# ScalarE scales the expert rows, the second half's selection is spread out, and the last chunk's second layer runs by tokens

## What is computed

```
scores = (tanh(xf @ gate_w.T) + 1) / 2
vals, idx = top_k(scores.T, k)              # k = 1028 rows for each of 8 experts
y = layernorm(xf[idx]) * gamma + beta       # rows of 256
h = gelu(y @ fc1s.T + b1s)                  # 1024 wide
o = (h @ fc2s.T + b2s) * vals               # back to 256
out = xf; out[idx] += o
```

## Time and profile before

| what | us |
|---|---|
| timed runs, median of 3 (lowest, highest) | 770.85 (768.74, 771.48) |
| the profiled execution | 768.64 |
| its span, first to last instruction | 766.8 |
| TensorE busy | 692.5 (90% of the span) |
| VectorE busy | 521.9 (68%) |
| ScalarE busy | 461.3 (60%) |
| GpSimd busy | 475.5 (62%) |

### The profile page before, as it was taken

One profiled execution on the slowest core, in us unless ns is written; L12 is line 12 of the kernel. 1 busy time (PEld: TensorE's weight loads), 2 busy tenths in 40 slices (PEclk: granted clock), 3 DMA queues, 4 the chain that ended last, 5 costly groups with the idle time before them and its releaser, 6 DMA issues.

```text
span 766.8 us, 15683 instructions
## 1 busy us (share of the span) xinstructions
PE 692.5 (90%) x4636; PEld 636.4 (83%) x4636; DVE 521.9 (68%) x1827; ACT 461.3 (60%) x1095; POOL 475.5 (62%) x660
## 2 busy tenths in 40 slices
PE   6988999999999963528899999999999999999994
PEld 3977788888888853518798999999999999999993
DVE  2855789989889867988767674766746756534431
ACT  1002588888888878706456566665675666756651
POOL 0248598889889645435166586575775856658323
PEclk9979999999999995559999999999999999999998
DMA  9910012222222228312143253253442443433122
GB/s 257 307 32 1 5 58 81 82 83 82 82 82 83 83 82 156 113 44 97 15 97 92 45 116 100 45 131 64 104 98 50 103 104 69 119 50 64 15 28 28
DMA packets 63568, 64.19 MB, mean 84 GB/s; under 512 B 14032, under 2 KB 57104, under 8 KB 63376
## 3 DMA queue, kind: packets, MB, share of 16 engines
q1 hardware_dynamic: 50576, 46.33, 20.6%
q0 software_dynamic: 12800, 17.12, 13.7%
q10 hardware_dynamic: 128, 0.00, 0.0%
HBM read 37.90 MB, written 25.53 MB: 83 GB/s over the span
## 4 chain that ended last, share of the span: by engine, by line
PE 50%; DVE 5%; ACT 4%; issue 1%; POOL 1%; DMA 0%; POOLq 0%; ACTq 0%; DVEq 0%
PE bank L1043 23%; PE bank L1057 16%; PE bank L1069 6%; PE bank L1030 3%; ACT bank L753 2%; PE bank L1020 1%; DVE jk L1605 1%; ACT jk L753 1%; PE bank L1080 1%; DVE yl L1624 1%; ACT bank L763 1%; ACT hh L766 0%; DVE hl L1630 0%; DMA yg<-rows,idx 0%; DVE bank L1617 0%
## 5 line engine op out<-in xcount | busy, mean ns | idle before, releaser
L584 POOL DMA_INDIRECT out<-ob,sidx x72 | 117.0, 1625 | 144.7 <-ACT ob L779 126.3
L1630 DVE TENSOR_TENSOR hl<-bank,hh 128x384 fp32r<-128x384 f32 (+1 forms) x192 | 98.1, 513 | 147.2 <-ACT hh L766 123.7
L763 ACT ACTIVATE bank<-bank,b1s 128x384 f32<-128x384 f32 (+1 forms) x192 | 99.6, 519 | 147.6 <-PE bank L1043 130.9
L1043 PE MATMUL bank<-yh,w1h 128*128 128x384 f32 (+1 forms) x384 | 131.0, 341 | 0.1
L1043 PE MATMUL bank<-yh,w1l 128*128 128x384 f32 (+1 forms) x384 | 122.9, 320 | 0.0
L1043 PE MATMUL bank<-yl,w1h 128*128 128x384 f32 (+1 forms) x384 | 122.5, 319 | 0.0
L1057 PE MATMUL bank<-w2h,hh 128*128 128x256 f32 x384 | 108.7, 283 | 0.0
L1057 PE MATMUL bank<-w2h,hl 128*128 128x256 f32 x384 | 108.4, 282 | 0.0
L1057 PE MATMUL bank<-w2l,hh 128*128 128x256 f32 x384 | 108.4, 282 | 0.0
L558 POOL DMA_INDIRECT yg<-rows,idx x72 | 71.1, 987 | 42.1 <-DVE idx L1608 22.2
L766 ACT ACTIVATE hh<-bank 128x384 fp32r<-128x384 f32 (+1 forms) x192 | 87.9, 458 | 6.1
(11 more groups left out here) (248 smaller groups left out, 1770.6 us busy)
## 6 DMA issues: line engine op xcount, KB each, us to landing
BIG<-in_x SPq DMA_DIRECT2D x4, 2048.0 KB, 16.1
out<-Bs SPq DMA_DIRECT2D x32, 256.0 KB, 2.2
rows<-Yp SPq DMA_DIRECT2D x32, 256.0 KB, 2.4
raw<-in_fc1T SPq DMA_DIRECT2D x16, 512.0 KB
raw<-in_fc2T SPq DMA_DIRECT2D x16, 512.0 KB
yg<-rows,idx POOLq DMA_INDIRECT x72
out<-ob,sidx POOLq DMA_INDIRECT x72
gwb<-in_gate_w SPq DMA_DIRECT2D x1, 1024.0 KB, 7.1
```

What stands on the lines that cost most here:

```text
L584: g.indirect_dma_start(out=out_rows, out_offset=tok(ap=sidx[job.eh][0:m, t:t + 1], axis=0), in_=ob[t % 3][0:m, :], in_offset=None, compute ...
L763: A.activation(h[:, 0:cur.w], h[:, 0:cur.w], ACT.Gelu_apprx_tanh, bias=b1s[:, bass.ds(cur.e, 1), f]).then_inc(s["hact"], 1)
L1043: last = T.matmul(Lb[ring(cur, f)][:, 0:cur.w], w1s[cur.eh][i][:, d, f * P:(f + 1) * P], yT[cur.p][k][:, d, 0:cur.w], start=(n == 0), stop ...
L1630: v.tensor_tensor(hT[cur.p][1][:, f, 0:cur.w], Lb[ring(cur, f)][:, 0:cur.w], hT[cur.p][0][:, f, 0:cur.w], ALU.subtract).then_inc(s["hlo"], 1)
```

## The change

ScalarE's `high_rows` now also scales (an Identity with a scale and a bias column per partition, in place in the bank, then a wait for it), and VectorE's `scaled` is gone. Ahead of job 0 VectorE takes the low rows after tile 6, not after tile 5. The selection of the second half is spread over jobs 1 to 3; TensorE's two steps of it go to the end of jobs 1 and 2, into bank 3, and the waits that guarded bank 7 move from `place` to the turns of jobs 3 and 4, which write bank 3. The last expert's third chunk has its second layer by tokens (72 matmuls, no transposes back); the third chunks of the other experts stay as they were.

```diff
...
                 self.half, self.group = (self.q // 4, self.q % 4) if isinstance(self.q, int) else (1, self.q - 4)
                 self.q_next = not (isinstance(self.q, int) and self.q == NE - 1)
                 self.t0, self.t1 = CHUNKS[self.c]
+                self.by_tokens = self.c < 2 or not self.q_next
                 self.w = sum(SLOTS[self.t0:self.t1])
         def place_bank(job, t):
...
         def second(prev, f):
-            cut = CUT[3 if prev.c < 2 else 2]
+            cut = CUT[3 if prev.by_tokens else 2]
             return [(n // len(TERMS), n % len(TERMS)) for n in range(cut[f - 1] if f else 0, cut[f])]
         def ring(job, f):
...
                 after(act, "hmm", (job.j - 1) * 8)
                 for d in range(2):
+                    act.wait_ge(s["yt_t"], job.j * 2 + d + 1)
+                    A.activation(bank[2 + d][:, 0:job.w], bank[2 + d][:, 0:job.w], ACT.Identity, scale=gam[:, d:d + 1],
+                                 bias=bet[:, d:d + 1]).then_inc(s["yr"], 1)
                     act.wait_ge(s["yr"], job.j * 2 + d + 1)
                     A.activation(yT[job.p][0][:, d, 0:job.w], bank[2 + d][:, 0:job.w], ACT.Copy).then_inc(s["yhi"], 1)
...
             def weighed(prev, t):
                 m = SLOTS[t]
-                if prev.c < 2:
+                if prev.by_tokens:
                     act.wait_ge(s["oadd"], prev.q * 6 + t + 1)
                     src = ot[t % 2][0:m, :]
                 else:
...
                         high(1 - cur.eh, cur.q + 1, cur.c // 2, WHIGH_AT.index(f))
                     if nxt and f == HIGH_AT:
                         high_rows(nxt)
-                    if prev and prev.c < 2 and f in OB_AT:
+                    if prev and prev.by_tokens and f in OB_AT:
                         weighed(prev, prev.t0 + OB_AT.index(f))
-                    if prev and prev.c == 2 and f == BACK_AT:
+                    if prev and not prev.by_tokens and f == BACK_AT:
                         for t in range(prev.t0, prev.t1):
                             weighed(prev, t)
             act.wait_ge(s["ld_par"], 112)
...
                     pe.wait_ge(s["oh_first" if split else "ohd"], job.q + 1)
                 if t == 3 and split:
                     pe.wait_ge(s["ohd"], 1)
-                if t == 6 and isinstance(job.q, int) and job.q == 1:
-                    pe.wait_ge(s["tk_read"], 2)
-                if t == 0 and isinstance(job.q, int) and job.q == 2:
-                    pe.wait_ge(s["tc"], 2)
                 after(pe, "smc", n - 1 if isinstance(job.q, int) and job.q == 0 else n)
                 T.matmul(place_bank(job, t)[0:m, 0:NT + 3], oh[:, t * P:t * P + m], TB[:, job.half, :], start=True,
...
             def turn(job):
                 after(pe, "yt", job.j * 2)
+                if at_job(job, 3):
+                    pe.wait_ge(s["tk_read"], 2)
+                if at_job(job, 4):
+                    pe.wait_ge(s["tc"], 2)
                 pe.wait_ge(s[f"gat{job.eh}{job.c}"], 48 * (job.el + 1))
                 for d in range(2):
                     for t in range(job.t0, job.t1):
...
                             for half in range(2):
                                 pe.wait_ge(s[f"wlo{half}"], prev.q * 2 + 2)
                         for u, n in second(prev, f):
-                            (token_term if prev.c < 2 else tail_term)(prev, u, n)
-                        if prev.c == 2 and f == BACK_AT:
+                            (token_term if prev.by_tokens else tail_term)(prev, u, n)
+                        if not prev.by_tokens and f == BACK_AT:
                             tail_back(prev)
                     if nxt and f == TURN_AT:
                         turn(nxt)
                     for tile in spread(tiles, f, 8):
                         place(*tile)
-                    if at_job(cur, 1) and f == 3:
-                        pe.wait_ge(s["smc"], 9 + 6)
-                        asked(1, bank[7])
-                    if at_job(cur, 2) and f == 0:
-                        pe.wait_ge(s["smc"], 2 * 9)
-                        begun(1, bank[7])
+                    if at_job(cur, 1) and f == 7:
+                        pe.wait_ge(s["yt"], nxt.j * 2 + 2)
+                        asked(1, bank[3])
+                    if at_job(cur, 2) and f == 7:
+                        pe.wait_ge(s["yt"], nxt.j * 2 + 2)
+                        begun(1, bank[3])
             pe.wait_ge(s["tc"], 1)
             for t in range(9):
                 place(Job(0, 0), t)
...
                 if t == 8 and job.q_next:
                     one_hot(Job(job.el, job.eh * 3 + 3))
-            def scaled(job):
-                for d in range(2):
-                    dve.wait_ge(s["yt_t"], job.j * 2 + d + 1)
-                    v.tensor_scalar(bank[2 + d][:, 0:job.w], bank[2 + d][:, 0:job.w], gam[:, d:d + 1],
-                                    bet[:, d:d + 1], ALU.mult, ALU.add).then_inc(s["yr"], 1)
             def low_rows(job):
                 for d in range(2):
...
                         low_hidden(cur, f)
                     if prev and f in OT_AT:
                         u = OT_AT.index(f)
-                        if prev.c < 2:
+                        if prev.by_tokens:
                             with_bias(prev, prev.t0 + u)
                         elif u < 2:
                             tail_bias(prev, u)
-                    if nxt and f == TURN_AT:
-                        scaled(nxt)
                     if nxt and f == LOW_AT:
                         low_rows(nxt)
                     if at_job(cur, 1) and f == 0:
                         above(1)
-                    if at_job(cur, 1) and f == 2:
+                    if at_job(cur, 1) and f == 3:
                         ranked_at(1)
-                    if at_job(cur, 1) and f == 4:
-                        asked_for(1, bank[7])
-                    if at_job(cur, 1) and f == 5:
+                    if at_job(cur, 2) and f == 0:
+                        asked_for(1, bank[3])
+                    if at_job(cur, 2) and f == 2:
                         taken(1)
-                    if at_job(cur, 1) and f == 7:
+                    if at_job(cur, 2) and f == 5:
                         ranked(1)
-                    if at_job(cur, 2) and f == 0:
+                    if at_job(cur, 2) and f == 7:
                         slots(1)
-                    if at_job(cur, 2) and f == 1:
-                        slots_of_images(1, bank[7])
+                    if at_job(cur, 3) and f == 0:
+                        slots_of_images(1, bank[3])
                     for tile in spread(tiles, f, 8):
                         place(*tile)
             dve.wait_ge(s["ld_par"], 112)
...
             one_hot(Job(0, 0), 3 * P, KTOK, "ohu", "ohd")
             for t in range(3, 9):
                 place(Job(0, 0), t)
-                if t == 5:
-                    scaled(Job(0, 0))
+                if t == 6:
                     low_rows(Job(0, 0))
             jobs(dve, emit)
```

## The result

| kernel | median us (lowest to highest, runs) | profiled execution | its span |
|---|---|---|---|
| before | 769.49 (768.38 to 771.48, 9) | 768.64 | 766.8 |
| after | 771.67 (770.84 to 772.66, 9) | 770.98 | 769.2 |

The ratio after to before is 1.0025, interval 1.0014 to 1.0037: some 1.9 us, small but measurable. The forecast was 771.0 us and no change.

The account below looks back on a forecast made before the run. TensorE was taken as the bound from about 360 to 749 us. Gains of 8.85 against stalls of 9.8 gave +0.9, 771.8 on the median, taken as 771.0 for clock falls in slower runs; own range 768.5 to 774.

Parts of the forecast that it names:

- start and job 0: At the start and in job 0 scaling leaves VectorE's chain, so job 1 gets its low rows earlier: -1.05 us.
- jobs 1 and 2 to the turn of job 3, clock included: The selection's TensorE waits there go or shrink (-1.1, -0.8, -1.85, and 0.15 behind); no clock fall, -1.65 us.
- job 2 step 3 to job 3: At the end of job 2 `begun` waits for `ranked`, now behind job 3's low rows: +0.25 us.
- tiles of step 6: In six jobs TensorE's one-hot tile waits for VectorE's tile of step 5, behind later low rows: +4.8 us.
- six first-to-second transitions: First chunk to second (jobs 6, 9, 12, 15, 18, 21): TensorE waits 0.84 us for low rows, together +5.0 us.
- jobs 7 and 13: Second-chunk jobs whose tile of step 4 waited behind VectorE's scaling; that wait goes: -0.5 us.
- tail: After the last matmul, last chunk by tokens: GpSimd's last issue at 759.2 in place of 761.19, -2.0 us.
- rival B: Faster: TensorE has more slack at the new stalls, which are half as long; 4.9 us less, 766 us; chance 0.18.
- A: Slower: ScalarE's `high_rows` grows by 0.2 to 0.4 us more at twelve places; about 775 us; chance 0.17.
- C: Much slower: Identity and gelu need different tables, two loads per job on ScalarE; 30 us, 800 us; chance 0.02.
- D: The tail does not shorten, the end hanging on a scatter's landing, not its issue; 773 us; chance 0.05.
- The clock: Half rate from 385.0 to 388.3 us, after the 1.84 us hole, taken not to recur: -1.65 us, between 0 and -3.3.

Follow-up runs that it names:

- the extra copy: The changed kernel with one more ScalarE copy of each bank of rows to a spare tile that nobody reads: 784.83 us, ratio to before 1.0213.
- the last variant: The kernel with only job 0 scaled by ScalarE and `taken` in step 0, with ScalarE also scaling the third chunks' rows: 760.09 us, ratio to before 0.9886.

## Why the prediction came out as it did

The time was within the range, a little above its middle, and the forecast of no change held. Against the terms (turns of the table, on the profiled executions):

| term | forecast | measured |
|---|---|---|
| already there at the turn of job 0 | none | −0.2 |
| start and job 0 | −1.05 | −0.8 |
| jobs 1 and 2 to the turn of job 3, clock included | −5.55 | −5.8 |
| job 2 step 3 to job 3 | +0.25 | +1.2 |
| tiles of step 6 (jobs 3, 5, 8, 11, 14, 17) | +4.8 | +4.7 |
| six first-to-second transitions | +5.0 | +5.6 |
| jobs 7 and 13 | −0.5 | −0.6 |
| tail | −2.0 | −1.7 |
| sum | +0.9 | +2.45 |

**What was right.** The mechanism of the twelve holes: ScalarE's 1.35 us reach TensorE through the gelu and VectorE's low rows. The scaling alone has all of them, the kernel with only job 0 on ScalarE does not wait for low rows after 400 us, and less for tiles (1.5 us) than the kernel before, and the extra copy lengthens each by its own length. That excludes rival B (slack). The six waits at tiles are 0.85 to 0.87 us in jobs 5, 8, 11, 14 and 17, and 1.61 in job 3; "over 1 us in jobs 5, 8 and 14", which was named as a sign, did not come. (The prediction's own figures for these six add up to 4.7, not 4.8.) The Identity at 0.64 and the rounds at 2.12 were measured at 0.639 and 2.11, which excludes A, and no table load came into the jobs (C). (The Trainium skill, ScalarE: Activation LUTs, What ACT_TABLE_LOAD costs, gives 0.69 by its price; the trace has 0.05 less, and the row of the gelu was the better guide.) The start was read rightly too: its tile comes with 0.76 us of idle time in place of the 2.25 of the earlier trace rows. From the turn of job 0 to that of job 1 it took 10.54, 11.33 and 11.40 us in the three executions with VectorE's scaling there, and 9.97 to 10.18 in the seven with ScalarE's and no further copy. The two slowest are those in which the granted clock rises to 1.00 last, at about 350 and 352 us, where it is 347.5 in the kernel before and 349 in the slowest of the seven. So the gain is there at a like clock, but its size is not known to better than some tenths of a us.

**Jobs 7 and 13, right by luck.** The prediction took this 0.5 out of the earlier trace rows, but the four waits of that row stand in jobs 3 (0.86 and 0.67 us), 11 and 17 (0.28 each). At the tiles of step 4 of jobs 7 and 13 only the weight load was idle, for 0.31 and 0.29 us. The kernel with the tail alone changed leaves VectorE's scaling there as it was, and it is 0.28 and 0.30 us shorter at the same two places. The profiled execution of the kernel before is the one that stands apart, so it is not shown that the move of the scaling gained anything here.

**Job 2, the term that failed.** I wrote that the eleven VectorE steps of the selection are the same, and looked only at where TensorE waits. I did not look at what GpSimd does in the step that `taken` moves into. There it subtracts weights, SBUF from SBUF. The kernel after, on VectorE, GpSimd and TensorE:

```profile
384.61 3.08 DVE L1547 TENSOR_TENSOR ge<-ge,eq 128x257 f32<-128x257 f32 x1
384.99 2.40 POOL L542 TENSOR_TENSOR w2l<-raw,w2h 128x1024 fp32r<-128x1024 f32 x1
388.99 0.28 PE L1022 MATMUL bank<-TB,oh 128*128 128x260 bf16 x1 [0.84 <-DVE jk L1611]
```

GpSimd ends at 387.39 and VectorE at 387.69. The hole is the tile's 0.84 in place of the 0.25 of `begun`. (The prediction also named "no wait of TensorE on the copy of tot" as a sign of being right, which its own 0.25 contradicts. There is none in this trace only because the tile's hole makes TensorE late; with `taken` early it is there, with 0.2.) Moving `taken` alone brought the instruction back to 0.43 us and took this hole away, so it is shown that the place makes it slow. Of the 1.2 us, 0.5 went with it; the rest are the wait of `begun` and its own two matmuls, which cost 0.26 where nothing waits (the kernel with only job 0 on ScalarE and `taken` early). That it is held by GpSimd rests on this: in the four kernels with `taken` in step 2 the two overlap, the instruction takes 3.08 or 3.09 us and ends 0.3 us after the subtraction; in the other seven they don't overlap, and it takes 0.43. No run took GpSimd's subtraction away. (The Trainium skill, SBUF — State Buffer, Who interferes with whom, says that a VectorE instruction with two SBUF inputs contends with a GpSimd instruction that reads SBUF, and calls the shared port pair "an exclusive lock". The trace agrees in that the VectorE instruction ends only after the whole subtraction, 0.30 us behind it.)

**The transitions** cost 0.84 to 0.98 each, four of them 0.98, and I had 0.84 for all. In job 9 TensorE begins 4.30 us after ScalarE's first instruction, before 3.43: that is 0.87, close to the forecast. The other 0.11 is the difference in length of the first matmul behind the hole: 0.44 us in place of 0.33. TensorE's idle time of 0.70 understates the price; the weight load's 1.03 is nearer to it.

**The tail** is 0.3 short of the forecast. No single step of it was wrong. ScalarE's row of the last tile is done 9.86 us after the first term, forecast 9.65, and the issue is at 10.74, forecast 10.5, in small handovers:

```profile
752.88 0.28 PE L1063 MATMUL bank<-w2h,hh 128*128 128x256 f32 x1
...
761.70 0.41 DVE L1642 TENSOR_TENSOR ot<-bank,b2b 4x256 f32<-4x256 f32 x1 [2.45 <-issue]
762.23 0.51 ACT L785 ACTIVATE ob<-ot,yg 4x256 f32<-4x256 f32 x1 [2.35 <-DVE ot L1642]
763.62 1.34 POOL L587 DMA_INDIRECT out<-ob,sidx  x1 [0.88 <-ACT ob L785]
```

From the last issue to the end of the span it is 5.6 us, as before, so D is excluded. (Two side figures of the prediction are off by its own numbers: GpSimd alone would give 753.5 + 2 x 1.87 = 757.2 for the last issue, −3.9 and not −4.1, and low rows at 357.1 in place of 358.06 give −0.96 for the start, not −1.05.)

**The clock** did not fall after 350 us in the profiled execution: where the earlier trace rows has 0.50, it is now

```profile
385.00:388.30 3.30, 3.16 (x28) 2.94 (x26) 3.27 (x4) 2.82 (x6) 3.13 (x2) 1.00 0.15 42
```

That rests on one execution. The other traces bear on it. Three kernels have the old selection and its hole of 1.84 to 1.86 us: the clock fell behind it in two of them (before, and the scaling alone), and not in the tail alone. Of the eight with the spread selection it fell in one, behind the 2.02 us of the kernel with only job 0 on ScalarE. The mean granted clock of whole executions points the same way. Of the 34 timed runs of the kernel before that stand beside the experiments, the 12 with 0.945 or less took 769.4 to 771.6 us, and the 22 with 0.947 or more took 767.4 to 769.9; the nine of the kernel after have 0.950 to 0.956. This fits the assumption that slower executions of the kernel before lose the clock more often, but a mean over an execution does not say where. How often it falls in either kernel stays open, and with it how much of the 1.65 the medians hold. I had taken 0.8 off the sum for slower executions of the kernel before. Without that the forecast would have been 771.8, nearer to the 771.67 measured, but by luck: the terms of the sum were short by 1.5.

**Where the gain went.** Of gains, 9.1 us were forecast, and the traces differ by 9.1 in these terms. Of that the 0.2 ahead of job 0 and the 0.6 at jobs 7 and 13 are not shown to be the change's, which leaves 8.3 from the start, jobs 1 and 2 and the tail, with 1.65 for the clock, as estimated, among them. The scaling of jobs 1 to 23 gave 10.3 us back at twelve places, and job 2 another 1.2. Keep the gains and leave those jobs on VectorE, with `taken` in step 0, and the kernel is 1.05% faster than before (0.9895, to which the last variant's 0.9886 adds nothing that can be measured).

## What to carry to other kernels

Work moved to an engine with idle time costs its length, less the slack there, wherever it stands in front of something that the bound engine will soon want: here 1.35 us more on ScalarE cost 0.84 to 0.98 at each transition, and 0.78 more on top of that cost 0.75. Ask of each such place how much slack there is, and try another step before another engine. When a step moves in time, list what every other engine does in the stretch that it enters, also those it shares no data with.

## What the hardware showed that was not expected

- One VectorE instruction of 257 columns with two SBUF inputs took 3.08 or 3.09 us in place of 0.43, in four kernels, each time beside a GpSimd subtraction of 2.40 or 2.41 us. By the recorded starts it was VectorE that began first, by 0.38 or 0.39 us, and it still ended last. Its mean over the two of that shape is 1752 ns in the kernel after, with the other one at its usual length, so only the timeline shows it.
- After holes of 2.02 us the granted clock fell to 0.50 (1.2 GHz) from 391.5 to 394.5 us in one execution and stayed at 1.00 in another; in the kernel before it fell after 1.84 us and not after 2.08, and in the tail alone not after 1.84. The length of the hole alone does not decide it.
- The first matmul behind a hole of 0.7 us took 0.41 to 0.44 us, in all six transitions, where it took 0.33 without one (job 9).
